# Expert rows packed without gaps: 16 gathers a pass in place of 23, tiles that start at a register's column, and a list of destinations fetched through memory

## The chip, the cores and the metric

The kernel runs on one core of one Trainium2 chip. The metric is the device time in microseconds of one execution. The kernel before takes 743.76 us (median of 3 runs, 742.2 to 744.45).

## The reference

Two sequences (batches) of 1024 rows of 128 numbers pass through six blocks, each with a layer norm in front and a residual after it: experts (344 wide, gated), RWKV time mixing, the same experts again, a second set of experts (512 wide, with biases), retention, and the second set again. Only the expert blocks are touched by the change:

```python
logits = xt @ Ws + bs
topk_w, topk_idx = jax.lax.top_k(logits, K)          # E = 8 experts, K = 2 of them for each row
topk_w = jax.nn.softmax(topk_w, axis=-1)
combine = jnp.sum(jax.nn.one_hot(topk_idx, E) * topk_w[..., None], axis=1)
g = jnp.einsum('td,edf->tef', xt, Wg)
u = jnp.einsum('td,edf->tef', xt, Wu)
y = jnp.einsum('tef,efd->ted', jax.nn.silu(g) * u, Wd)
out = jnp.einsum('ted,te->td', y, combine)
```

The kernel computes only the two chosen experts of each row: 2 x 1024 pairs of row and expert in each batch.

## The kernel before

Four expert blocks (f = 0, 2, 3, 5) times two batches (b) make eight **passes**, numbered 0 to 7: (0,0), (0,1), (2,0), (2,1), (3,0), (3,1), (5,0), (5,1). Passes 0 to 3 are of the gated kind (k = 0), 4 to 7 of the other (k = 1). A pass sorts the 2048 pairs by expert and cuts them into **tiles** of 128 places with one expert each. Each expert begins a new tile, so that a pass needs up to 16 + 7 = 23 tiles (`TILES`), some of whose places are empty.

- **Routing** (`route`, mostly VectorE): logits, the two best experts, a running count, a slot for each pair. A one-hot product on TensorE (step `inv`) turns "pair to slot" into "slot to row". VectorE makes three lists of it: `te` (the expert of each tile), `take_from` (the row for each place) and `send_to` (where each result goes in DRAM; empty places go to spare rows there).
- **Gathering**: GpSimd issues one indirect DMA for each tile (`rows_in`, L1089), DRAM `rows_in` to SBUF `xs`. TensorE transposes the rows in groups (`transpose_in`, L562) of 1, 2, 4, 4, 4, 4, 4 tiles, and ScalarE copies each group from PSUM to `xT_kept` (`copy_x`, L872).
- **A tile**: ScalarE copies the tile's weights (`copy_w`, L865), TensorE multiplies up (`project_up`, L590), ScalarE applies silu, and in passes 0 to 3 VectorE multiplies gate and value into `hT` (`product`, L1304). TensorE multiplies down (`project_down`, L602), and two tiles at a time are copied from one PSUM bank to `ys` (`copy_y`: by ScalarE in passes 0 to 3, L899; by VectorE in passes 4 to 7, L1315). `hT`, the gate and the up banks are double, the down bank `ybank` is single.
- **Sending**: one indirect DMA a tile by GpSimd (`rows_out`, L1103) to DRAM `rows_out`. `ys` holds eight tiles. When a pass is all sent, SyncE reads the results back in eight DMAs (`rows_back`, L449), and VectorE adds them to x with the weights `cw` (`add`, L1390).

The batches leapfrog: while the tiles of one batch run, the other's adds, norm, mixing and routing run beside them. Each engine has one fixed order, written out as a string in `TURNS`: each letter is a program of the engine (`a` is always the tiles, but on SyncE and GpSimd), and `a3` means three steps of it. Nothing overtakes anything on an engine: a step whose semaphore is late holds up all that stands behind it. On TensorE, `load_owner` reads the expert of tile j + 2 from `te` into a register at the head of tile j; ScalarE reads it right before it copies the weights:

```python
load_owner(PASSES[p][1], j)
e = act.snap(owners[j % len(owners)], min_val=0, max_val=E - 1)
nc.scalar.activation(w_up[:, n % 2, 0:UP[k]], w_of(k, e, 0, UP[k]), ACT.Copy).then_inc(w_copied, 1)
```

Of the kernel before, what the change touches and what calls it, by code (L numbers as in the profile page):

```python
# [38 lines left out]
assert OPENS[NG] == TILES  # L39
# [47 lines left out]
    "act":  # L87
# [4 lines left out]
    "pool":  # L92
# [4 lines left out]
    "dve":  # L97
# [47 lines left out]
def build_block(nc, x_in, w0_in, w1_in, cols_in, sq_in, gn_in, const_in, bconst_in, bias_in, rope_in, decay_in, out):  # L145
    ctx = ExitStack()
    with ctx:
# [9 lines left out]

        x = sb("x", [P, NB * NT, P])
# [16 lines left out]
        xnT = sb("xnT", [P, NB, 1 + S])  # L175
        zT = sb("zT", [P, NB, S])
# [12 lines left out]
        gap = sb("gap", [P, 2, NT])  # L189
        tiles_i = sb("tiles_i", [P, E], I32)  # L190
        tiles = sb("tiles", [P, 3, E])
# [6 lines left out]
        of_tile = sb("of_tile", [P, K * NT, NSB], F16)  # L198
        from_row = sb("from_row", [P, K * NT, NSB], F16)
        unused = hot = sb("unused", [P, NSB])  # L200
        row_i = sb("row_i", [P, NSB], I32)
        take_from = sb("take_from", [P, NB, NSB], I32)
        send_to = sb("send_to", [P, NB, NSB], I32)
        count = sb("count", [P, P + K * NT + NSB])
# [170 lines left out]
        def group_after(p, j):  # L375

            q, t = place(p, j)
            if t != max(0, filled(q % NG) - 2) or q % NG == NG - 1 and p in DRAINED:
                return None
# [1363 lines left out]
```

## Time and profile before

| | |
|---|---|
| the profiled execution | 741.35 us, its span 739.4 us, mean granted TensorE clock 0.925 |
| runs | 742.2, 743.76, 744.45 us |
| TensorE (PE) busy | 607.4 us, 82% of the span |
| ScalarE (ACT), GpSimd (POOL), VectorE (DVE) busy | 424.0, 406.3 and 402.1 us |
| moved by DMA | 51.50 MB, mean 70 GB/s |

Times in the trace count from the start of the span. "idle before <-releaser" on a row is the time in which the engine had nothing to do before it, and what ended that time. `SPq` is SyncE, which only issues DMAs. In the timeline, the second number of an issue is how long the issuing engine was taken, not how long the data were under way; the latter stands in the list of DMA issues.

### The profile page before, as it was taken

The page shows a single profiled execution, that of the slowest core. Times are in us where ns is not written, and L with a number is a line of the kernel's source. Part 1 is how long each engine was busy: PE and PEld are TensorE (multiplying, and loading weights), DVE is VectorE, ACT ScalarE, POOL GpSimd, SP SyncE. Part 2 cuts the span into 40 slices and gives each one's busy share as a digit, 9 for nine tenths or more (in the row PEclk, how much of TensorE's full clock was granted, in tenths as well). Part 3 has the DMA queues.
Part 4 walks back from the last instruction along what each step waited for, and adds up shares of the span by engine and source line. Part 5 has one row for each costly group of instructions (what it writes and reads, how often), then busy time and mean ns, then how long its engine had stood idle before and what let it go on. Part 6 is the DMA issues. An engine that isn't in the chain of part 4 may idle for free.

```text
span 739.4 us, 14790 instructions
## 1 busy us (share of the span) xinstructions
PE 607.4 (82%) x4780; PEld 517.1 (70%) x4780; DVE 402.1 (54%) x1253; ACT 424.0 (57%) x1014; POOL 406.3 (55%) x436
## 2 busy tenths in 40 slices
PE   2489959869496997998998889997439999888891
PEld 1489959569366987997988776665336667678891
DVE  5663236856769771672445334586672576660302
ACT  2156637776269754765867676452227454646870
POOL 2167767633657537766776776322038534326773
PEclk9999989969698999999999999999559999998996
DMA  8842231101310213321421311000311001102423
GB/s 342 319 138 54 53 108 47 33 16 51 96 40 23 45 47 89 97 56 44 112 80 43 111 48 34 8 9 16 89 15 43 26 9 30 51 15 51 137 51 111
DMA packets 42617, 51.50 MB, mean 70 GB/s; under 512 B 7848, under 2 KB 33832, under 8 KB 42416
## 3 DMA queue, kind: packets, MB, share of 16 engines
q0 software_dynamic: 11776, 24.14, 12.5%
q1 hardware_dynamic: 30768, 26.41, 10.9%
q8 instruction: 43, 0.70, 0.4%
q14 instruction: 30, 0.25, 0.1%
HBM read 33.22 MB, written 17.30 MB: 68 GB/s over the span
## 4 chain that ended last, share of the span: by engine, by line
PE 52%; POOL 15%; DVE 10%; issue 9%; ACT 7%; DMA 6%; ACTq 0%; SPq 0%; POOLq 0%; DVEq 0%
PE bank L590 19%; PE bank L602 11%; POOL xs L1089 9%; POOL rows_out L1103 7%; PE bank L692 5%; DMA xs<-rows_in,take_from 3%; PE bank L714 2%; PE bank L562 2%; PE bank L670 2%; PE bank L527 2%; DVE in_tile L1266 2%; DMA rows_out<-ys,send_to 1%; PE bank L516 1%; ACT xn L822 1%; ACT L822 1%
## 5 line engine op out<-in xcount | busy, mean ns | idle before, releaser
L590 PE MATMUL bank<-xT_kept,w_up 128*128 128x128 f32 x1840 | 257.5, 290 | 25.5 <-ACT gate L880 8.6
L1103 POOL DMA_INDIRECT rows_out<-ys,send_to x184 | 182.4, 991 | 151.4 <-DVE ys L1315 58.1
L590 PEld LDWEIGHTS bank<-xT_kept,w_up 128*128 128x128 f32 x1840 | 234.1, 202 | 40.1 <-issue 29.7
L1089 POOL DMA_INDIRECT xs<-rows_in,take_from x184 | 180.9, 983 | 126.3 <-issue 49.3
L602 PE MATMUL bank<-w,hT 128*128 x1288 | 182.6, 283 | 14.9 <-DVE ys L1315 8.6
L602 PEld LDWEIGHTS bank<-w,hT 128*128 128x128 f32 x1288 | 164.5, 197 | 24.1 <-issue 23.8
L865 ACT ACTIVATE w_up<-w 128x728 f32 (+1 forms) x184 | 133.0, 725 | 28.1 <-DVE cw L1290 7.6
L887 ACT ACTIVATE hT<-bank,tile_bias 128x128 f32<-128x128 f32 x368 | 104.9, 370 | 45.2 <-PE bank L590 43.4
L1304 DVE TENSOR_TENSOR hT<-gate,bank 128x384 f32<-128x384 f32 x92 | 50.4, 550 | 86.2 <-ACT gate L880 53.2
L872 ACT ACTIVATE xT_kept<-bank 128x512 f32<-128x512 f32 (+2 forms) x56 | 29.2, 522 | 78.9 <-PE bank L562 78.8
L1315 DVE COPY ys<-bank 128x256 f32<-128x256 f32 (+1 forms) x48 | 19.7, 411 | 97.8 <-PE bank L605 81.8
L1539 DVE TENSOR_TENSOR kept<-bank,decay 128x512 f32<-128x512 f32 x64 | 41.4, 685 | 38.1 <-PE bank L692 38.1
L880 ACT ACTIVATE gate<-bank 128x384 f32<-128x384 f32 x92 | 44.4, 483 | 17.1 <-PE bank L590 15.1
L562 PE MATMUL bank<-const,xs 128*128 128x128 f32 x184 | 33.9, 297 | 21.8 <-DMA xs<-rows_in,take_from 21.5
L1390 DVE SCALAR_TENSOR_TENSOR x<-yg,cw,x 128x128 f32<-128x128 f32 x128 | 37.4, 340 | 25.5 <-DMA yg<-rows_out 25.4
L506 PE MATMUL bank<-const,xn 128*128 128x128 f32 x96 | 22.2, 339 | 22.1 <-DVE xn L1191 21.3
L562 PEld LDWEIGHTS bank<-const,xs 128*128 128x128 f32 x184 | 23.1, 152 | 24.3 <-issue 16.2
L692 PE MATMUL bank<-kept 32*128 32x512 f32 x128 | 37.0, 640 | 0.0
L899 ACT ACTIVATE ys<-bank 128x256 f32<-128x256 f32 (+1 forms) x48 | 17.9, 373 | 31.2 <-PE bank L602 30.8
L506 PEld LDWEIGHTS bank<-const,xn 128*128 128x128 f32 x96 | 14.5, 166 | 27.5 <-issue 20.5
L822 ACT ACTIVATE kept<-bank 128x128 f32<-128x128 f32 (+1 forms) x36 | 12.0, 332 | 33.2 <-PE bank L681 21.9
L1167 DVE BATCH_NORM_STATS2 stats<-x 128x6 f32<-128x128 f32 x96 | 26.1, 277 | 8.4 <-DMA colv<-in_vectors 6.3
(160 smaller groups left out, 708.1 us busy)
## 6 DMA issues: line engine op xcount, KB each, us to landing
yg<-rows_out SPq DMA_DIRECT2D x64, 128.0 KB, 2.9
w<-in_w SPq DMA_DIRECT2D x8, 536.0 KB, 10.4
rows_in<-xn SPq DMA_DIRECT2D x16, 256.0 KB, 2.4
w<-in_w SPq DMA_DIRECT2D x8, 512.0 KB, 8.7
xs<-rows_in,take_from POOLq DMA_INDIRECT x184, 3.0
rows_out<-ys,send_to POOLq DMA_INDIRECT x184
x<-in_x SPq DMA_DIRECT2D x2, 512.0 KB, 5.6
decay<-in_decay SPq DMA_DIRECT2D x1, 1024.0 KB, 13.2
```

What stands on the lines that cost most here:

```text
L562: last = nc.tensor.transpose(xT[:, t * P:(t + 1) * P], xs[:, q % 2, t, :], ident)
L590: last = mm(to, w_up[:, n % 2, start_col:start_col + P], rows_in, start=True, stop=True)
L602: last = mm(y, hT[0:n_f, n % 2, c * P:(c + 1) * P], w_of(k, e, WD[k] + c * P, P, n_f), start=(c == 0), stop=(k == 0 and c == CH[k] - 1))
L692: mm(to[:], r_kT[quad, c % 2, :], r_qm[quad, c % 2, :, :].rearrange("p a b -> p (a b)"), start=True, stop=True).then_inc(RE_PE.sem, 1)
L865: nc.scalar.activation(w_up[:, n % 2, 0:UP[k]], w_of(k, e, 0, UP[k]), ACT.Copy).then_inc(w_copied, 1)
L880: nc.scalar.activation(gate[:, n % 2, :], bank[0][:, 0:CH[0] * P], ACT.Silu).then_inc(gate_ready, 1)
L887: last = nc.scalar.activation(hT[:, n % 2, c * P:(c + 1) * P], bank[up_bank(p, j)][:, c * P:(c + 1) * P], ACT.Silu, bias=own)
L1089: pool.indirect_dma_start(xs[:, q % 2, t, :], None, xn_dram[b], own).then_inc(ld_xs[q % 2][t], 16)
L1103: pool.indirect_dma_start(y_dram[b], own, ys[:, m % 4 // 2, m % 2 * 2 + j % 2, :], None)\
L1304: V.tensor_tensor(hT[:, n % 2, 0:CH[0] * P], gate[:, n % 2, :], bank[up_bank(p, j, 1)][:, 0:CH[0] * P], ALU.mult)\
L1390: V.scalar_tensor_tensor(row, yg[:, s, t, :], cw[:, b, s, t:t + 1], row, ALU.mult, ALU.add)\
L1539: step(V.tensor_tensor(r_A[:, c % 2, q * HALF:(q + 1) * HALF], score[q % 2][:], decay[:, q * HALF:(q + 1) * HALF], ALU.mult))
```

## The change

1. **No gaps.** Slots are counted without rounding each expert up, so the 2048 pairs of a pass fill exactly 16 blocks of 128 rows (`ROWS`): 16 gathers a pass, and groups of 1, 3, 4, 4, 4. `xT_kept` goes. ScalarE copies each transposed group into `turned`, 2048 columns and 128 zeros behind them for each batch, in the place of `xnT` and `zT`.
2. **Tiles stay at 23**, but overlap blocks: the tile's 128 columns begin where a new list `off` says. TensorE reads `off` into a register beside `te`, and `project_up` takes `turned[:, b, register : register + 128]`. A pass's tiles wait for `off`, made some steps after `te`.
3. **Destinations.** `send_to` can no longer be read off `inv` in tile order. VectorE writes the rows of the 16 blocks out as numbers (`row_f`), TensorE transposes them (a fourth routing step, `turn`), VectorE copies the result (`row_t`), SyncE writes it to DRAM (`place_dram`), waits, and then for each of the 23 tiles reads `off` into a register and issues a DMA of 128 numbers of 4 bytes, one for each partition, into `places[:, b, j]`. VectorE waits for all 23 and makes `send_to` of them with two operations.
4. **Routing on VectorE** loses three small operations ahead of the slots and gets some fifteen behind them. `gap`, `hot` and `unused` are double by batch.
5. **The orders** of all five engines are written anew.

```diff
-GROUPS = [1, 2] + [GRP] * ((TILES - 3) // GRP)
+ROWS = K * S // P
+GROUPS = [1, 3] + [GRP] * ((ROWS - 4) // GRP)
...
     "sp":
-        "a3 c3 a2 b9 a2 b8 a2 b8 a2 b8 a2 b16 a4 b8 d5 b8 d4",
+        "a3 d3 a2 b5 c9 a2 c8 b2 a2 b2 c8 a2 b2 c8 a2 b2 c16 a2 b2 a2 b2 c8 e5 c8 e4",
...
+            def places_by_tile():
+                for p, (f, b) in enumerate(PASSES):
+                    steps = RT_DVE[b]
+                    yield
...
+                    sp.wait_ge(steps.sem, steps.done(SUB[f], "row_t"))
+                    sp.dma_start(place_dram[b][1:1 + K * S].rearrange("(t p) -> t p", p=P), row_t[0:ROWS, b, :]).then_inc(places_out[b], 16)
+                    yield
...
+                    sp.wait_ge(places_out[b], 16 * (SUB[f] + 1))
+                    for j in range(TILES):
+                        own = offs[j % len(offs)]
+                        sp.reg_load(own, off[0:1, b * NSB + j:b * NSB + j + 1])
+                        first = sp.snap(own, min_val=1, max_val=1 + K * S)
+                        sp.dma_start(places[:, b, j:j + 1], place_dram[b][bass.ds(first, P)].unsqueeze(1)).then_inc(places_back[b], 16)
...
             def load_owner(b, j):
                 pe.reg_load(owners[j % len(owners)], te[0:1, b * NSB + j:b * NSB + j + 1])
+                pe.reg_load(offs[j % len(offs)], off[0:1, b * NSB + j:b * NSB + j + 1])
...
-                if t == 0:
-                    pe.wait_ge(xT_copied, q + 1)
+                if j in OPENS[0:NG]:
+                    pe.wait_ge(xT_copied, p * NG + OPENS.index(j) + 1)
                 pe.wait_ge(w_copied, n + 1)
-                rows_in = xT_kept[:, q % 2, t * P:(t + 1) * P]
+                first = pe.snap(offs[j % len(offs)], min_val=1, max_val=1 + K * S)
+                rows_in = turned[:, PASSES[p][1], bass.ds(first, P)]
...
-                    for j in range(TILES):
+                    for j in range(ROWS):
                         yield
                         q, t = place(p, j)
...
-                step(V.scalar_tensor_tensor(send_to[:, b, :], row_i[:], 0.0, unused[:], ALU.add, ALU.add))
+                step(V.scalar_tensor_tensor(unused[:, b, :], full[:, b, :], 0.0, count[:, P + K * NT:], ALU.is_equal, ALU.mult))
+                yield
+
+                dve.wait_ge(places_back[b], 16 * TILES * (v + 1))
+                after(R, v, "unused")
+                step(V.tensor_tensor(full[:, b, :], full[:, b, :], places[:, b, :], ALU.mult))
+                after(R, v, "kept")
+                step(V.tensor_tensor(send_to[:, b, :], full[:, b, :], unused[:, b, :], ALU.add))
                 yield
```

The orders of VectorE, spelled out from the new string around the two steps that matter (`row_t` is the copy that lets SyncE write the list; `SEND` is the wait for all 23 DMAs with its two operations; P3.1 is the product of tile 1 of pass 3, Y4.10 the copy of the eleventh pair of pass 4, A a step of adding, N the norm):

| pass | what stands between `row_t` and `SEND` | what follows `SEND` |
|---|---|---|
| 0 | set-up, first steps of the next routing, P0.0, P0.1 | next routing, P0.2 |
| 1 | P0.10, set-up, P0.11, P0.12 | P0.13 |
| 2 | ten adds, P2.0, P2.1, a norm, P2.2 | P2.3, RWKV of batch 1 |
| 3 | P2.22, P3.0 | P3.1 |
| 4 | P3.21, P3.22 | residual, A of pass 3 (four steps), Y4.0 |
| 5 | Y4.9 | Y4.10 |
| 6 | two adds, a norm | residual, first rotation of retention of batch 1 |
| 7 | Y6.10, Y6.11 | residual, Y7.0 |

`row_t` itself follows the routing closely (passes 0, 2, 6, 7: right behind `take_from` and `off`; pass 3: behind P2.20 and P2.21; pass 5: behind Y4.8; pass 1: behind P0.8 and P0.9; pass 4: behind P3.19 and P3.20). In GpSimd's new order the sends of a pass begin behind 12 to 16 of its gathers, as they began behind 11 to 15 before.

## Rows read from the trace of the kernel before

**Rows 1.** The page: chain that ended last, and costliest groups (busy us, mean ns)
```profile
PE bank L590 19%; PE bank L602 11%; POOL xs L1089 9%; POOL rows_out L1103 7%; PE bank L692 5%; DMA xs<-rows_in,take_from 3%; PE bank L714 2%; PE bank L562 2%; PE bank L670 2%; PE bank L527 2%; DVE in_tile L1266 2%; DMA rows_out<-ys,send_to 1%; PE bank L516 1%; ACT xn L822 1%; ACT L822 1%
...
L1103 POOL DMA_INDIRECT rows_out<-ys,send_to x184 | 182.4, 991 | 151.4 <-DVE ys L1315 58.1
...
L1089 POOL DMA_INDIRECT xs<-rows_in,take_from x184 | 180.9, 983 | 126.3 <-issue 49.3
...
L562 PE MATMUL bank<-const,xs 128*128 128x128 f32 x184 | 33.9, 297 | 21.8 <-DMA xs<-rows_in,take_from 21.5
```

**Rows 2.** Timeline of POOL, the last send of pass 0
```profile
98.73 0.97 POOL L1103 DMA_INDIRECT rows_out<-ys,send_to  x1 [0.30 <-issue]
```

**Rows 3.** Busy time by stretch: PE, PEld, DVE, ACT, POOL, clock, DMA share, GB/s
```profile
100.00:110.00 10.00, 4.96 (x22) 4.12 (x23) 4.72 (x19) 1.79 (x3) 6.83 (x7) 0.66 0.57 158
```

**Rows 4.** Timeline of SP: start, us for all of them, count
```profile
28.48 0.44 SPq L462 DMA_DIRECT2D decay<-in_decay  x1
...
101.12 3.95 SPq L449 DMA_DIRECT2D yg<-rows_out  x8
...
353.62 4.58 SPq L449 DMA_DIRECT2D yg<-rows_out  x8
```

**Rows 5.** DMA issues: KB each, median us from issue to landing
```profile
rows_in<-xn SPq DMA_DIRECT2D x16, 256.0 KB, 2.4
...
decay<-in_decay SPq DMA_DIRECT2D x1, 1024.0 KB, 13.2
```

**Rows 6.** Timeline of DVE, then ACT: the list te, and the copy that reads it
```profile
543.61 0.17 DVE L1276 TENSOR_SCALAR te<-owner 128x24 int32<-128x24 f32 x1
...
544.23 0.63 ACT L865 ACTIVATE w_up<-w 128x512 f32 x1 [7.50 <-DVE te L1276]
```

**Rows 7.** Timeline of DVE at the start of pass 0
```profile
31.61 0.18 DVE L1283 TENSOR_SCALAR take_from<-row_i 128x24 int32<-128x24 int32 x1
...
45.30 0.55 DVE L1304 TENSOR_TENSOR hT<-gate,bank 128x384 f32<-128x384 f32 x1 [0.91 <-PE bank L590]
...
49.65 0.55 DVE L1304 TENSOR_TENSOR hT<-gate,bank 128x384 f32<-128x384 f32 x1
```

**Rows 8.** Timeline of DVE in pass 0, the first and last of six products
```profile
62.20 0.55 DVE L1304 TENSOR_TENSOR hT<-gate,bank 128x384 f32<-128x384 f32 x1 [1.31 <-PE bank L590]
...
73.00 0.55 DVE L1304 TENSOR_TENSOR hT<-gate,bank 128x384 f32<-128x384 f32 x1 [1.69 <-ACT gate L880]
```

**Rows 9.** Timeline of DVE at the starts of passes 2 and 3
```profile
191.23 0.18 DVE L1283 TENSOR_SCALAR take_from<-row_i 128x24 int32<-128x24 int32 x1
...
209.21 0.55 DVE L1304 TENSOR_TENSOR hT<-gate,bank 128x384 f32<-128x384 f32 x1 [2.42 <-ACT gate L880]
...
275.25 0.18 DVE L1283 TENSOR_SCALAR take_from<-row_i 128x24 int32<-128x24 int32 x1
...
286.76 0.56 DVE L1304 TENSOR_TENSOR hT<-gate,bank 128x384 f32<-128x384 f32 x1 [3.60 <-PE bank L590]
```

**Rows 10.** Timeline of DVE around the starts of passes 4 and 5
```profile
337.93 0.56 DVE L1304 TENSOR_TENSOR hT<-gate,bank 128x384 f32<-128x384 f32 x1 [0.26 <-ACT gate L880]
...
354.14 0.42 DVE L1315 COPY ys<-bank 128x256 f32<-128x256 f32 x1 [11.63 <-PE bank L605]
...
398.17 0.18 DVE L1283 TENSOR_SCALAR take_from<-row_i 128x24 int32<-128x24 int32 x1
...
405.65 0.42 DVE L1315 COPY ys<-bank 128x256 f32<-128x256 f32 x1 [3.43 <-PE bank L605]
```

**Rows 11.** Timeline of DVE around the starts of passes 6 and 7
```profile
545.99 0.18 DVE L1283 TENSOR_SCALAR take_from<-row_i 128x24 int32<-128x24 int32 x1
...
557.10 0.76 DVE L1530 TENSOR_TENSOR kept<-bank,rope 128x256 f32<-128x256 f32 x2 [4.96 <-PE bank L670]
...
663.42 0.18 DVE L1283 TENSOR_SCALAR take_from<-row_i 128x24 int32<-128x24 int32 x1
...
679.29 0.42 DVE L1315 COPY ys<-bank 128x256 f32<-128x256 f32 x1 [4.80 <-PE bank L605]
```

More of the change, by code:

```diff
@@ L156, in build_block @@
         y_dram = [nc.dram_tensor(f"rows_out{b}", [K * S + NSB * P, P], F32).ap() for b in range(NB)]
+        place_dram = [nc.dram_tensor(f"places{b}", [1 + K * S + P], I32).ap() for b in range(NB)]
         x = sb("x", [P, NB * NT, P])
@@ L197, in build_block @@
         in_tile = sb("in_tile", [P, K * NT, P], F16)
[L198 to L202, printed above, removed]
+        of_tile = sb("of_tile", [P, K * NT, ROWS], F16)
+        from_row = sb("from_row", [P, K * NT, ROWS], F16)
+        unused = hot = sb("unused", [P, NB, NSB])
+        full = sb("full", [P, NB, NSB])
+        none_of = sb("none_of", [P, E + 1])
+        reach = sb("reach", [P, NSB, E])
+        row_i = sb("row_i", [P, ROWS], I32)
+        row_f = sb("row_f", [P, ROWS])
+        row_t = sb("row_t", [P, NB, P], I32)
+        places = sb("places", [P, NB, NSB], I32)
+        take_from = sb("take_from", [P, NB, ROWS], I32)
         send_to = sb("send_to", [P, NB, NSB], I32)
@@ L307, in build_block @@
                         ["lg", "top0", "eq0", "nth0", "pick0", "rest", "top1", "eq1", "nth1", "pick1", "sel", "carry",
-                         "gap", "tile127", "tiles_i", "tiles", "end", "start", "slot", "mine", "pos", "slot_i", "tile", "in", "eq", "rows", "in0", "in1",
-                         "ended", "owner", "te", "unused", "row_i", "take", "send", "w0", "w1"]) for b in range(NB)]
+                         "gap", "end", "start", "slot", "mine", "pos", "slot_i", "tile", "in", "eq", "rows", "in0", "in1",
+                         "tile127", "tiles_i", "tiles", "last", "ended", "owner", "te", "row_i", "take", "row_f",
+                         "none", "pad", "ahead", "padded", "less", "at", "off", "row_t", "more", "sum", "reach", "full", "unused", "kept", "send",
+                         "w0", "w1"]) for b in range(NB)]
         RES = [Steps(sem(f"res{b}"), [f"res{i}" for i in range(NH)]) for b in range(NB)]
@@ L375, in group_after @@
         def group_after(p, j):
-            q, t = place(p, j)
-            if t != max(0, filled(q % NG) - 2) or q % NG == NG - 1 and p in DRAINED:
-                return None
-            return q + 1
-        def last_tile(q):
-            return q // NG * TILES + OPENS[q % NG + 1] - 1
+            if j == TILES - 2 and p not in DRAINED:
+                return (p + 1) * NG
+            for g in range(1, NG):
+                if j == max(OPENS[g] - 2, OPENS[g - 1]):
+                    return p * NG + g
+            return None
         def up_made(n, part=0):
@@ L484, in _ @@
             owners = [pe.alloc_register(f"owner{i}") for i in range(6)]
+            offs = [pe.alloc_register(f"off{i}") for i in range(4)]
             ident = const[:, K_ID:K_ID + P]
@@ L519, in route @@
                 own = 6 if (f, b) == (5, 0) else 7
-                to = take(own, RT_DVE[b], v, "send")
+                to = take(own, RT_DVE[b], v, "more")
                 for t in range(NT):
@@ L855, in route @@
                 after(RT_DVE[b], v, "gap")
[L856 removed]
+                run(gap[:, b, 1, :], gap[:, b, 0, :], ACT.Tanh, RT_ACT[b], scale=0.5)
             def copy_w(p, j):
@@ new lines, in route @@
+                yield
+                step(V.tensor_tensor(none_of[:, 0:E], start_of, end_of, ALU.subtract))
+                after(R, v, "none")
+                step(V.scalar_tensor_tensor(pad_of, tiles_of, float(P), none_of[:, 0:E], ALU.mult, ALU.add))
+                after(R, v, "pad")
+                step(V.tensor_tensor(more_of, pad_of, none_of[:, 1:E + 1], ALU.subtract))
+                step(V.tensor_tensor(reach[:, :, :], ended[:, :, :], pad_of.unsqueeze(1).to_broadcast([P, NSB, E]), ALU.mult))
@@ new lines, in route @@
+                after(R, v, "padded")
+                after(R, v, "te")
+                step(V.tensor_reduce(owner[:], reach[:, :, :], AX.X, ALU.add))
+                after(R, v, "less")
+                step(V.scalar_tensor_tensor(owner[:], const[:, K_J:K_J + NSB], float(P), owner[:], ALU.mult, ALU.subtract))
+                after(R, v, "at")
+                step(V.tensor_scalar(off[:, b * NSB:(b + 1) * NSB], owner[:], float(K * S), 1.0, ALU.min, ALU.add))
+                yield
+                after(RT_PE[b], v, "turn")
@@ L1284, in route @@
+                step(V.tensor_copy(row_t[0:ROWS, b, :], own[0:ROWS, 320:320 + P]))
                 if k == 1:
                     V.tensor_copy(tile_bias[:, b, :, :], heads(own[:, 192:192 + CH[1] * NSB], CH[1], NSB)).then_inc(TB_DVE[b].sem, 1)
-                step(V.scalar_tensor_tensor(send_to[:, b, :], row_i[:], 0.0, unused[:], ALU.add, ALU.add))
+                step(V.tensor_tensor(reach[:, :, :], ended[:, :, :], more_of.unsqueeze(1).to_broadcast([P, NSB, E]), ALU.mult))
+                after(R, v, "more")
@@ new lines, in route @@
+                step(V.tensor_reduce(owner[:], reach[:, :, :], AX.X, ALU.add))
+                after(R, v, "sum")
+                step(V.scalar_tensor_tensor(owner[:], const[:, K_J:K_J + NSB], -float(P), owner[:], ALU.mult, ALU.add))
+                after(R, v, "reach")
+                step(V.tensor_scalar(full[:, b, :], owner[:], none_of[:, 0:1], count[:, P:P + 1], ALU.subtract, ALU.is_ge))
+                after(R, v, "full")
+                step(V.scalar_tensor_tensor(unused[:, b, :], full[:, b, :], 0.0, count[:, P + K * NT:], ALU.is_equal, ALU.mult))
@@ L1289, in route @@
                 for s, sign in enumerate((0.25, -0.25)):
-                    step(V.tensor_scalar(cw[:, b, s, :], gap[:, 1, :], sign, 0.25, ALU.mult, ALU.add))
+                    step(V.tensor_scalar(cw[:, b, s, :], gap[:, b, 1, :], sign, 0.25, ALU.mult, ALU.add))
                 if k == 1:
```

101 lines of the change are left out of this document (61 added, 40 removed), and 39 rows, old and new, of the table TURNS.

## Prediction

> **What bounds the kernel now.** I read the page first. TensorE is busy for 82% of the span and no other engine for more than 57%, but the chain that ended last gives the tiles' matmuls only 30% and GpSimd's two indirect DMAs 16% [rows 1]. A gather or a send costs GpSimd 0.98 or 0.99 us [rows 1] and 0.30 us before the next, 1.27 us in a row [rows 2]; a pass has 46 of them, 58 us, against some 50 us of tile work on TensorE (23 tiles at 2.16 us: the six products between 62.20 and 73.00 lie five tiles apart [rows 8]). So GpSimd falls behind in a pass without other work, and the next pass's gathers come late: between 100 and 110 us TensorE works 4.96 of 10 us and its granted clock is 0.66 in place of 1 [rows 3]. The reader is to see two things: GpSimd's backlog is real but hurts only at the ends of passes, and the tiles run on a pace of about 2 us, set by TensorE with ScalarE and VectorE in the loop. Whatever stops VectorE for longer than one tile stops the tiles (its product fills `hT`, or its copy frees the single `ybank`).
>
> **What the change takes away.** 56 of 184 gathers: 56 x 1.27 = 71 us of GpSimd. Of this only what lies on the chain counts. Gathers have 9% of the chain, 66 us, and 56/184 of that is 20; transposes have 2%, 15 us, and 56/184 of that is 4.5 [rows 1]. Together **24 us gained**. The bounds: the gap at 100 to 110 us alone, 5 us [rows 3], and all 71 us. I take 24, since TensorE is close to full outside such gaps. The copies to `turned` are fewer than those to `xT_kept`, but ScalarE waits beside TensorE. The lost operations ahead of the slots (three of some 0.2 us, as `te` with its gap [rows 6]) are given back by the four of `te` that moved behind `in1`; `off` comes some 1.7 us behind `take_from`, while the first tile waits for a gather, a transpose and a copy anyway: nothing, and 1.7 us a pass if that cover were gone.
>
> **What it adds: the way of the destinations.** From `row_t` to `SEND` this stands in a row, and nothing of it overlaps:
> - the write to DRAM, from issue to landing: 2.4 us, as the stores of `rows_in` [rows 5];
> - 23 times a register load and a DMA issue on SyncE. Eight issues take 3.95 us [rows 4], 0.49 us each. These have static addresses. The load: `te` ends at 543.78 and ScalarE, which waits for it, reads it into a register and starts its copy at 544.23 [rows 6], 0.45 us with the semaphore and the start, so about 0.4. The load and the issue that needs it are in order on one queue, so I take 0.9 us an entry: 0.4 + 22 x 0.9 = 20.2 us to the last issue. The bounds: 0.49 (the load hidden behind the issue), and 1.25 (a slower load, and arithmetic of a dynamic address, which no row shows);
> - the last one's landing: 2.4 us by the same row.
>
> The sum is **25 us from `row_t` to `SEND`**, 16 by the lower bound, 33 by the upper. The rows show a register load of about 0.4 us on ScalarE [rows 6]. The Trainium skill, "DMA: Bandwidth & Descriptors", section "Latency and other measured facts", puts a tensor_load at a floor of about 600 ns; with that an entry would be 1.09 us, the way 29 us, and the total below some 30 us higher.
>
> What is queued behind it: VectorE's wait for all 23 DMAs stands in its one order, a few steps behind `row_t`. Behind it stand the products and copies of the running pass, for which TensorE waits within one or two tiles, and GpSimd's sends. How much each pass loses is the time at which its next step can run, less the time at which it ran before:
> - **Pass 0**: `take_from` is done at 31.8 [rows 7], `row_t` about 33.5. The list is on SyncE's queue behind the weights of the other experts and `decay`, issued at 28.48 and landed 13.2 us later, 41.7 [rows 4, 5]. The write lands behind them, about 42; 42 + 20.2 + 2.4 = 64.6, P0.2 at some 65.5 in place of 49.65 [rows 7]: 16 us.
> - **Pass 1**: three products, 6.5 us by [rows 8], lie between `row_t` and `SEND`; P0.13 would be due 2.2 us later: 25 - 8.7 = 16 us.
> - **Pass 2**: `take_from` + 2 + 25 = 27 us; P2.3 came at 209.21, 18 us behind 191.23 [rows 9]: 9 us.
> - **Pass 3**: + 2.5 + 25 = 27.5; P3.1 came 11.5 us behind `take_from` [rows 9]: 16 us.
> - **Pass 4**: `row_t` behind P3.20 (337.93 [rows 10]), so `SEND` at 363.5. SyncE reads pass 3 back only behind its list, at 361 in place of 353.62 [rows 4], and Y4.0 stands behind four of those adds: 367 in place of 354.14 [rows 10]: 13 us. TensorE idled for a part of those 12 us before as well.
> - **Pass 5**: + 3 + 25 = 28; Y4.10 came 7.5 us behind `take_from` [rows 10]: 20.5 us. Pass 4's last sends, its reading back and so retention of batch 0 come as much later.
> - **Pass 6**: + 2 + 25, and 1.5 for the residual = 28.5; the first rotation of retention came 11.1 us behind `take_from` [rows 11]: 17.5 us.
> - **Pass 7**: 28.5 as well; Y7.0 came 15.9 us behind [rows 11]: 12.5 us.
>
> The sum is 16 + 16 + 9 + 16 + 13 + 20.5 + 17.5 + 12.5 = **120.5 us lost**. They add, since each stops tiles or the chain of the next routing, and all eight lie one behind the other in time. Parts that I cost at nothing: the second register load a tile on TensorE (0.4 us x 184 = 74 us if its queue runs dry, and the tile pace of rows 8, which has one such load, leaves no gap), the tile's start at an odd column, and 2,944 packets of 4 bytes a pass, 184 for each of 16 DMA engines in 20 us. VectorE's some fifteen small operations at 0.2 us are 3 us a pass, mostly beside waits. GpSimd's sends start up to 10 us later than its order has them, but its 39 DMAs (50 us) fit into a pass that is now longer.
>
> **Sum**: 120.5 - 24 = 96.5 us on the profiled execution's 741.35: 838 us. The median of the runs shown is 2.4 us above that execution: **840 us**. A change of 0.3% (2.2 us) is about what a measurement of this kernel can tell from none.
>
> **The rivals.**
> - *The load hides behind the issue* (25%). SyncE's sequencer goes on while an issue is being worked off, an entry costs 0.49, and `SEND` comes 16 us behind `row_t`. Each of the eight losses is 9 us less: 7, 7, 0, 7, 4, 11.5, 8.5, 3.5 = 48.5; less 24 is +25: **768 us**. For it: the issues of 0.49 us show no work of their own in the trace beyond the 0.43 of the issue. Against: the next issue can't form its address before its register is there.
> - *More than forecast* (10%). The entry is 1.25 us or TensorE's second load shows: 7.7 us more in eight places, 62 us: **900 us**.
> - *Faster: the list is short* (12%). The one mechanism that decides the sign is SyncE's time per entry. The new order of VectorE puts `SEND` only 4 to 6 us behind `row_t` (three products in pass 1), which fits a list whose issues cost next to nothing. If small transfers can be handed over at 0.06 us each, `SEND` waits hardly anywhere, and the 24 us remain: **719 us**. It decides below 0.37 us an entry: 96.5/8 = 12 us less of the 25. Against it stands that every issue of SyncE takes 0.44 to 0.57 us whatever its size [rows 4]. By the Trainium skill, same page, section "Anatomy of one DMA", a sequencer hands a DMA over in some 50 ns; that is said of GpSimd's way, and on SyncE this trace has 0.49 us.
> - *The gain is larger* (with the 25% above it would reach no change, 5%): if not 24 but some 50 of GpSimd's 71 us come back, and an entry is 0.49 us, it ends near **743 us**.
>
> **How the numbers follow.** The forecast's own case, an entry of 0.75 to 1.1 us, has 48% and runs from 815 to 880. The range takes in the hidden load and goes up to the upper bound of an entry: 762 to 900, which leaves out the fast list, most of the larger gain, and what lies above 900. Faster: 12% and half of the last, 14%. Same: 3%. Slower: 83%.
>
> **What would show it.** In the new trace's timeline of SP, 23 issues of `places` a pass: their distance is the entry (0.9 us; 0.5 for the first rival; 0.1 for the fast list). VectorE should stand idle before the operation that makes `full` out of `places`, released by the DMA `places`, eight times and some 100 us in all; 16 to 19 us in passes 0 and 1. TensorE should stand in the same stretches at the lower clock. GpSimd should show 128 gathers, idle before the first send of a pass, and no more gap at the start of pass 1 by late gathers. The prediction is wrong if VectorE finds the list there, or if tiles go on while it waits (then the losses don't add), and its size is wrong if entries are not 0.9 us.

## The result and the profile after

The changed kernel takes **847.71 us** (median of 4 runs, 845.68 to 850.25) beside 742.98 us (4 runs, 742.2 to 744.45) for the kernel before on the same chip: ratio **1.141**, 95% interval 1.137 to 1.145. It is slower by 105 us. The forecast was 840 us, its range 762 to 900.

The page of the changed kernel (busy time, clock, the chain that ended last, costliest groups):

```profile
span 845.6 us, 15852 instructions
...
PE 630.9 (75%) x4732; PEld 532.9 (63%) x4732; DVE 422.3 (50%) x1375; ACT 417.7 (49%) x998; POOL 352.3 (42%) x381
...
PE 50%; SPq 17%; DVE 10%; issue 8%; ACT 7%; DMA 6%; ACTq 0%; POOL 0%; POOLq 0%; DVEq 0%
PE bank L634 19%; PE bank L646 13%; SPq L470 8%; SPq L468 6%; PE bank L736 4%; DMA places<-row_t 2%; PE bank L758 2%; ACT hT L932 2%; PE bank L714 2%; DMA places<-places 2%; PE bank L565 1%; DVE in_tile L1310 1%; ACT xn L866 1%; PE bank L60
...
L1149 POOL DMA_INDIRECT rows_out<-ys,send_to x184 | 185.6, 1009 | 289.4 <-DVE ys L1401 116.4
...
L1135 POOL DMA_INDIRECT xs<-rows_in,take_from x128 | 123.6, 966 | 106.5 <-DVE none_of L1339 57.4
...
L1370 DVE TENSOR_TENSOR full<-full,places 128x24 f32<-128x24 f32 x8 | 1.5, 183 | 125.8 <-DMA places<-places 125.8
...
L605 PE MATMUL bank<-const,xs 128*128 128x128 f32 x128 | 24.7, 308 | 6.2 <-DMA xs<-rows_in,take_from 4.8
```

Three things are to be seen beside [rows 1]. GpSimd has left the chain (gathers and sends had 16%, now POOL has 0%), and the transposes wait for gathers for 4.8 us in place of 21.5: what the change was to relieve is relieved. (The list stretches this kernel and so gives GpSimd time as well; the run with one entry a pass, below, shows the same without it, 1% and 4.4 us.) SyncE, which had no share of the chain, has 17%: L468 is the register load of a list entry, L470 its DMA. And one operation of 0.18 us, L1370, which stands behind VectorE's wait for the list, has 125.8 us of idle time ahead of it.

The timeline of SP shows the eight lists (start, us for all 23, count):

```profile
44.36 18.74 SPq L470 DMA_DIRECT2D places<-places  x23
...
85.88 19.06 SPq L470 DMA_DIRECT2D places<-places  x23
...
226.21 18.79 SPq L470 DMA_DIRECT2D places<-places  x23
...
323.02 18.08 SPq L470 DMA_DIRECT2D places<-places  x23
...
395.40 19.54 SPq L470 DMA_DIRECT2D places<-places  x23
...
466.85 18.64 SPq L470 DMA_DIRECT2D places<-places  x23
...
629.56 19.32 SPq L470 DMA_DIRECT2D places<-places  x23
...
764.39 18.60 SPq L470 DMA_DIRECT2D places<-places  x23
```

They sum to 150.8 us, 18.85 a list. From the first issue's start to the last one's end are 22 distances and one issue of 0.33 us: (18.85 - 0.33) / 22 = 0.84 us an entry on average, and 0.81 in the shortest list, the fourth (18.08 us). The chain through pass 1's list shows what an entry is made of (start, us, what):

```profile
84.06 1.37 DMA places<-row_t
85.88 0.34 SPq L470
...
91.28 0.33 SPq L470
91.66 0.32 SPq L468
92.13 0.33 SPq L470
...
104.61 1.97 DMA places<-places
107.16 0.47 DVE hT L1390
```

A load takes 0.27 to 0.32 us and an issue 0.33. From an issue's end to the next load are 0.04 us, from a load's end to its issue 0.16, in which the trace has L469, the `snap` of the register, for 0.04 and a first piece of L470 for 0.03. The next load begins only when the issue has ended. From the write at 84.06 to the last landing at 106.58 are 22.5 us. TensorE in the midst of such a wait (stretch; PE, PEld, DVE, ACT, POOL busy; clock, DMA share, GB/s):

```profile
100.00:110.00 10.00, 2.23 (x10) 2.23 (x11) 1.44 (x6) 0.51 (x2) 0.00 (x0) 0.50 0.05 1
```

TensorE works 2.23 of 10 us, at a granted clock of 0.50, the lower of its two levels (1.2 GHz), and GpSimd does nothing. In pass 0 the order of VectorE behind the list reads:

```profile
64.75 0.18 DVE L1370 TENSOR_TENSOR full<-full,places 128x24 f32<-128x24 f32 x1 [17.67 <-DMA places<-places]
64.97 0.18 DVE L1372 TENSOR_TENSOR send_to<-full,unused 128x24 int32<-128x24 f32 x1
...
66.51 0.55 DVE L1390 TENSOR_TENSOR hT<-gate,bank 128x384 f32<-128x384 f32 x1
```

The forecast had `SEND` (L1370 and L1372) at 64.6 and P0.2 (L1390) at 65.5. That it fits so well is in part luck: the first issue came at 44.36, 2 us later than forecast (42.4), and the list and its landing were 1.8 us shorter. `row_t` was ready at 33.1, but SyncE wrote it only at 37.61, since an issue ahead of it (L458, the zeros behind the list in DRAM, which the forecast left out) held SyncE for 3.67 us.

### The profile page after: what moved, and what is told of

Its sections match the earlier page's. It is cut to its first block, busy times and chain, and to the rows that moved or that the text cites. A ratio compares the mean times of both kernels' runs of the same rounds, so it can differ in the third digit from the quotient of the medians.

```text
span 845.6 us, 15852 instructions
## 1 busy us (share of the span) xinstructions
PE 630.9 (75%) x4732; PEld 532.9 (63%) x4732; DVE 422.3 (50%) x1375; ACT 417.7 (49%) x998; POOL 352.3 (42%) x381
## 4 chain that ended last, share of the span: by engine, by line
PE 50%; SPq 17%; DVE 10%; issue 8%; ACT 7%; DMA 6%; ACTq 0%; POOL 0%; POOLq 0%; DVEq 0%
PE bank L634 19%; PE bank L646 13%; SPq L470 8%; SPq L468 6%; PE bank L736 4%; DMA places<-row_t 2%; PE bank L758 2%; ACT hT L932 2%; PE bank L714 2%; DMA places<-places 2%; PE bank L565 1%; DVE in_tile L1310 1%; ACT xn L866 1%; PE bank L605 1%; PE bank L554 1%
## 5 line engine op out<-in xcount | busy, mean ns | idle before, releaser
L1149 POOL DMA_INDIRECT rows_out<-ys,send_to x184 | 185.6, 1009 | 289.4 <-DVE ys L1401 116.4
L634 PE MATMUL bank<-turned,w_up 128*128 x1840 | 269.8, 298 | 34.9 <-ACT gate L925 11.4
L634 PEld LDWEIGHTS bank<-turned,w_up 128*128 128x128 f32 x1840 | 242.7, 208 | 56.9 <-issue 55.1
L646 PE MATMUL bank<-w,hT 128*128 x1288 | 193.2, 294 | 76.6 <-DVE ys L1401 37.9
L646 PEld LDWEIGHTS bank<-w,hT 128*128 128x128 f32 x1288 | 175.3, 208 | 84.8 <-issue 84.1
L1135 POOL DMA_INDIRECT xs<-rows_in,take_from x128 | 123.6, 966 | 106.5 <-DVE none_of L1339 57.4
L1390 DVE TENSOR_TENSOR hT<-gate,bank 128x384 f32<-128x384 f32 x92 | 50.2, 551 | 71.0 <-PE bank L634 41.8
L1370 DVE TENSOR_TENSOR full<-full,places 128x24 f32<-128x24 f32 x8 | 1.5, 183 | 125.8 <-DMA places<-places 125.8
L917 ACT ACTIVATE turned<-bank 128x512 f32<-128x512 f32 (+2 forms) x40 | 20.6, 514 | 75.0 <-PE bank L605 69.4
L1176 POOL TENSOR_TENSOR kept<-kept 128x256 f32<-128x256 f32 x16 | 11.6, 726 | 58.2 <-DVE kept L1619 58.1
L605 PE MATMUL bank<-const,xs 128*128 128x128 f32 x128 | 24.7, 308 | 6.2 <-DMA xs<-rows_in,take_from 4.8
```

Source lines behind the costliest of these rows:

```text
L634: last = mm(to, w_up[:, n % 2, start_col:start_col + P], rows_in, start=True, stop=True)
L646: last = mm(y, hT[0:n_f, n % 2, c * P:(c + 1) * P], w_of(k, e, WD[k] + c * P, P, n_f), start=(c == 0), stop=(k == 0 and c == CH[k] - 1))
L1135: pool.indirect_dma_start(xs[:, q % 2, t, :], None, xn_dram[b], own).then_inc(ld_xs[q % 2][t], 16)
L1149: pool.indirect_dma_start(y_dram[b], own, ys[:, m % 4 // 2, m % 2 * 2 + j % 2, :], None)\
L1390: V.tensor_tensor(hT[:, n % 2, 0:CH[0] * P], gate[:, n % 2, :], bank[up_bank(p, j, 1)][:, 0:CH[0] * P], ALU.mult)\
```

## The experiments

Twelve runs were made, in three groups, each group with the kernel before on the same chip. The first group's chip gave 741.61 us for the kernel before (median of 13), beside 742.98 in the first measurement. The other two groups fell on two other chips, on which the kernel before takes 881.44 us (median of 7) and 882.92 us (median of 11). Times are therefore compared within a group only, with one exception: the changed kernel did not run in the first group, and its 847.71 us are taken from the first measurement, where the kernel before differs by 0.2%. "The first chip" below means both.

The kernels with fixed addresses, with one entry a pass and with fixed columns leave out the destinations: `send_to` is a fixed count in them, so that results go to consecutive rows of DRAM and not to their own. With fixed columns the tiles hold other rows too. The others compute all.

### First group: what the list costs

**Fixed addresses.** The list's DMAs stay, the load of the register goes, and with it the address made of it:

```diff
-                        own = offs[j % len(offs)]
-                        sp.reg_load(own, off[0:1, b * NSB + j:b * NSB + j + 1])
-                        first = sp.snap(own, min_val=1, max_val=1 + K * S)
-                        sp.dma_start(places[:, b, j:j + 1], place_dram[b][bass.ds(first, P)].unsqueeze(1))...
+                        first = 1 + j % ROWS * P
+                        sp.dma_start(places[:, b, j:j + 1], place_dram[b][first:first + P].unsqueeze(1))...
...
-                step(V.tensor_tensor(send_to[:, b, :], full[:, b, :], unused[:, b, :], ALU.add))
+                step(V.tensor_scalar(send_to[:, b, 0:TILES], count[:, P:P + TILES], -1.0, None, ALU.add))
```

> The 23 DMAs of the list have fixed addresses, with no register load in front of them; VectorE still waits for all 23. The destinations are then not the tiles' own: the sends go to fixed rows, so the output is scrambled. Theory (an entry of the list, now 0.82 us, is a register load and an issue one behind the other, and every microsecond of it is paid in each of eight passes): the entry falls to the 0.49 us of the other issues, each wait is 7.2 us shorter, the time falls by some 57 us to about 790 us. Rival (the handing over of small DMAs is slow by itself): entries stay at 0.8 us and the time at 848 us.

Measured: 789.17 us, ratio 1.065 (1.056 to 1.074), 58.5 us below the changed kernel. VectorE's wait, from the view of waits (us in total, times, longest):

```profile
DVE full L1368 <- DMA places<-places: 68.6, 8, 11.8
```

Its eight lists sum to 93.1 us, 57.7 fewer than the 150.8 (an issue every 0.51 us: 11.63 less 0.43, over 22), and the kernel is 58.5 us faster: what a list gains the kernel gains, one for one, and the fixed destinations, which this run has as well, are left with at most 1 us. The register load does not hide behind the issue.

**One entry a pass.** `range(TILES)` becomes `range(1)`, VectorE waits for that one, and the destinations are fixed as in the run before:

```diff
-                    for j in range(TILES):
+                    for j in range(1):
...
-                dve.wait_ge(places_back[b], 16 * TILES * (v + 1))
+                dve.wait_ge(places_back[b], 16 * (v + 1))
```

> The list is one DMA a pass in place of 23; destinations fixed as in the first run, so the output is scrambled. All else of the change stays: packed gathers, the transposes, the write to memory and its landing, VectorE's added operations. Theory: of the 125.8 us that VectorE waits, each wait loses up to 18 us, so nearly all; what remains is the gain by 56 fewer gathers, about 24 us: some 720 to 725 us, faster than the kernel before. Rival (a part of the loss is the added operations or the second register load of TensorE): it ends above 743 us.

Measured: 740.37 us (10 runs), ratio 0.999 (0.995 to 1.003). VectorE's wait for the list is 3.0 us in all. Without the rest of the list the whole change makes no difference that can be measured. The other 22 entries of the eight lists cost 847.7 - 740.4 = 107.3 us, and the gain of the packing, forecast at 24 us, is missing: the 720 to 725 us expected here did not come.

**The list twice.** 46 entries a pass, the second half into a second buffer, and VectorE waits for all:

```diff
-                    for j in range(TILES):
+                    for i, j in enumerate([*range(TILES), *range(TILES)]):
...
-                        sp.dma_start(places[:, b, j:j + 1], ...
+                        sp.dma_start((places, places2)[i >= TILES][:, b, j:j + 1], ...
...
-                dve.wait_ge(places_back[b], 16 * TILES * (v + 1))
+                dve.wait_ge(places_back[b], 16 * 2 * TILES * (v + 1))
```

> The list is fetched twice (46 DMAs, the second 23 into a tile that nobody reads), and VectorE waits for all 46. Theory: 23 x 0.82 = 18.7 us more in each of eight passes, all of it added: 150 us more, about 998 us. Rival (passes overlap or other waits absorb a part): clearly under 120 us more.

Measured: 998.22 us, ratio 1.347, 150.5 us above the changed kernel. Its eight lists sum to 301.3 us, 150.5 more than the changed kernel's: the same number. The view of waits:

```profile
DVE full L1371 <- DMA places<-places: 275.7, 8, 38.1
```

149.9 us more than the 125.8. Nothing absorbs even a part of the second half. Of the first half a little is absorbed: from one entry to 23 the lists grow by 147.8 us and the kernel by 107.3, so that some 5 us a list cost nothing, and every entry beyond is on the path.

**The wait on GpSimd.** VectorE no longer waits. GpSimd waits for the list just ahead of the first send of a pass, and makes `send_to` itself with four small operations, in place of VectorE's:

```diff
-                dve.wait_ge(places_back[b], 16 * TILES * (v + 1))
-                after(R, v, "unused")
-                step(V.tensor_tensor(full[:, b, :], full[:, b, :], places[:, b, :], ALU.mult))
...
+                            pool.wait_ge(places_back[b], 16 * TILES * (SUB[f] + 1))
+                            nc.gpsimd.tensor_copy(place_f[:, b, :], places[:, b, :])...
+                            nc.gpsimd.tensor_tensor(full[:, b, :], full[:, b, :], place_f[:, b, :], ALU.mult)...
+                            nc.gpsimd.tensor_tensor(full[:, b, :], full[:, b, :], unused[:, b, :], ALU.add)...
+                            nc.gpsimd.tensor_copy(send_to[:, b, :], full[:, b, :])...
```

> The wait for the list and the making of send_to move from VectorE to GpSimd, right in front of a pass's first send; the list is as slow as before, and every order stays. Theory (what costs is that VectorE's products and copies stand behind the wait): tiles run on while the list is fetched, eight of them find room; GpSimd's gathers and retention steps behind its first send still come late, some 5 to 10 us in passes 0, 5 and 6: 750 to 775 us. Rival (the late destinations hold up the sends and so the pass, whoever waits): 830 us or more.

Measured: 778.47 us, ratio 1.052 (1.044 to 1.060). The lists are as long as before:

```profile
44.38 18.96 SPq L472 DMA_DIRECT2D places<-places  x23
```

So 69 of the 107 us are owed to who waits for the list: VectorE's wait stops products and copies that have nothing to do with destinations. 38 us stay, and GpSimd waits 42.3 us for the list. The time lies 3.5 us above the upper end of the expected 750 to 775.

### Second group: finer waits, and TensorE's second load

**The list in three parts** (8, 8 and 7 entries), each with its own semaphore, and GpSimd waits for a part at the first send that uses it:

```diff
-                        ....then_inc(places_back[b], 16)
+                        ....then_inc(places_part[b][j // 8], 16)
...
+                        if j % 8 == 0:
+                            pool.wait_ge(places_part[b][c], 16 * (min(j + 8, TILES) - j) * (SUB[f] + 1))
```

> As the wait on GpSimd, which measured 778.5 us and let GpSimd wait 42 us for lists, but the list is taken in three parts of 8, 8 and 7 entries: GpSimd waits for the first eight before the first send, 2.4 + 8 x 0.82 + 2.4 = 11 us behind row_t in place of 24. Theory: the wait of GpSimd all but vanishes and the time comes to that of the one-entry list and some small operations: 742 to 752 us. Rival (SyncE's queue being full is the cost: reading back stands behind the list): it stays at 765 us or more.

Measured: 851.40 us beside 881.44, ratio 0.966 (0.961 to 0.971). GpSimd's wait for the list is down to 6.8 us, once, and SyncE has 4% of the chain. The wait all but vanished, as the theory had it; the expected times were those of the first chip and can't be set beside this one. The time does not come to that of one entry a pass, which is 822 to 826 us on this chip with fixed columns.

**A fixed column, without and with the second load** (both have one entry a pass). TensorE reads its tiles from fixed columns. The first drops the load of `off` (the line taken out below), the second keeps it and doesn't use it:

```diff
-                pe.reg_load(offs[j % len(offs)], off[0:1, b * NSB + j:b * NSB + j + 1])
...
-                first = pe.snap(offs[j % len(offs)], min_val=1, max_val=1 + K * S)
-                rows_in = turned[:, PASSES[p][1], bass.ds(first, P)]
+                first = 1 + j % ROWS * P
+                rows_in = turned[:, PASSES[p][1], first:first + P]
```

> The one-entry list (740.4 us), and TensorE's tiles start at fixed columns, with no second register load a tile; the output is scrambled. The one-entry run gained 2 us in place of the 24 expected of the packed gathers; its trace shows 82 short stops of TensorE's weight loads ahead of the up products, 55 us in all, where the kernel before had 42 and 30 us. Theory A (the second register load costs TensorE 0.1 to 0.2 us a tile): 715 to 725 us. Theory B (what ate the gain is VectorE's fifteen added operations in the routing, and the order): 738 to 741 us.

> As the run before, but TensorE still loads the second register for each tile and does not use it. Theory A (the load costs, not the column that starts at an odd place): 740 us. Rival (reading from a register's column costs): as fast as the run without load.

Measured: 822.18 us without the load, ratio 0.933 (0.928 to 0.939), and 826.02 us with it, 0.936 (0.931 to 0.941). The intervals overlap: the 3.8 us between the two are within the noise, and the 184 loads don't cost 74.

**Four loads ahead of four issues** on SyncE, in the otherwise unchanged new kernel:

```diff
+                        for j in some:
+                            sp.reg_load(offs[j % len(offs)], off[0:1, b * NSB + j:b * NSB + j + 1])
+                        for j in some:
+                            first = sp.snap(offs[j % len(offs)], min_val=1, max_val=1 + K * S)
+                            sp.dma_start(places[:, b, j:j + 1], ...
```

> The changed kernel whole, with one edit: SyncE loads four registers in a row and then issues their four DMAs, in place of load, issue, load, issue. Theory (loads run one into the next, and four cost little more than one, 0.33 us): an entry falls from 0.82 to some 0.57 us, 23 entries by 5.6 us, the time by 8 x 5.6 = 45 us to about 803 us. Rival (each load takes its 0.33 us wherever it stands): 848 us.

Measured: 919.50 us, ratio 1.043 (1.037 to 1.049). The trace shows why the expected 45 us didn't come: where nothing disturbs SyncE, four loads start at 103.77, 104.07, 104.36 and 104.66 us, 0.30 apart, their four issues at 105.10, 105.62, 106.14 and 106.65, 0.52 apart, and the next load at 107.02. Four entries take 3.25 us, the same 0.81 us each. The changed kernel itself had not run on a chip of this speed, so it did in the next group.

### Third group: the open sizes on one chip

> The changed kernel itself, beside the others of this call, so that all are compared on one chip. Theory (the list costs 0.815 us an entry on the path): 1.141 times the kernel before, as in the first measurement (848 us beside 743). Where the chip is one on which the kernel before takes about 881 us, the run with four loads ahead of four issues had 1.043; the changed kernel should stand at 1.04 to 1.06 there.

> The changed kernel with one list entry a pass and fixed destinations for the scatters (the rows land in other places than the reference's). Theory (packing the tiles is worth about 2 us and the list all the rest): 0.997 to 1.003 times the kernel before, 740 us where that takes 742. Rival (packing is worth more and the first run of it missed it): 0.97 to 0.98.

> As the run before, and TensorE reads each tile from a fixed column, with no second register load (so the tiles hold other rows too). Theory (the register's column costs TensorE little, as the 4 us between the two runs with and without the load say): 0.5% below the run before, 736 us. Rival (a start in an odd or register-given column slows each transpose, and this took the 24 us that the packing was forecast to give): 3% below, about 718 us. The run tells the two apart, since it differs from the one before in nothing else.

> The whole change computed in full, with the list in three parts (8, 8 and 7 entries) that GpSimd waits for just ahead of the scatters that use them, and SyncE's register loads four ahead of four issues. Theory (VectorE's wait is gone, and what stays is SyncE's and GpSimd's own path): the run with the wait on GpSimd for all 23 had 778 us; by thirds the first scatter waits for 8 entries and not 23, 12 us less in each of 7 passes at most, of which GpSimd shows 42 us of wait in all: 742 to 760 us, 1.00 to 1.025 times the kernel before. With the loads by four an entry costs no less if the 0.815 us are 0.49 of issue and 0.33 of load one after the other (22 x 0.815 = 18 us a list); rival: the loads overlap, and a list takes 22 x 0.5 = 11 us, which would put the time near 740.

The edits are those above; the last one joins the three parts and the loads by four.

| kernel | us | ratio to the kernel before (882.92) | 95% |
|---|---|---|---|
| changed | 920.76 | 1.041 | 1.035 to 1.046 |
| one entry a pass | 826.49 | 0.938 | 0.934 to 0.942 |
| the same, fixed columns, no second load | 827.62 | 0.936 | 0.931 to 0.940 |
| three parts on GpSimd, loads by four | 853.15 | 0.966 | 0.961 to 0.971 |

What follows:
- Loads by four are worth nothing that can be measured: 1.043 beside 1.041, and 0.966 with them beside 0.966 without, each pair on two chips of the same speed. Load and issue add up in either order.
- The register's column and the second load cost TensorE nothing in time (826.49 and 827.62). They do leave a trace: the short stops "issue" ahead of the weight loads of the up products are 87.9 us with the column from a register and 66.3 with a fixed one. On the first chip they are 29.7 us in the kernel before and 55.2 with one entry a pass; there no run had fixed columns, so that a cost of the register's column is not excluded where the 24 us are missing.
- The list costs 920.76 - 826.49 = 94 us here, much as the 107 us on the first chip. Moved to GpSimd in parts it costs 853.15 - 826.49 = 27. Of these GpSimd waits 7.0 us for the list, and its own small operations keep it busy for 24 us more (378.3 beside 353.9); what the rest is was not separated. The run came out below its expected ratio of 1.00 to 1.025, which took the first chip's times for its base.
- The forecast of 0.997 to 1.003 for one entry a pass failed, and so did its rival's 0.97 to 0.98. The same kernel that equals the kernel before on the first chip is 6% faster than it here.

The last point is about the chips. One entry a pass, on the first chip and on this one, from the two pages and views of waits. First chip:

```profile
span 738.6 us, 15148 instructions
...
L634 PE MATMUL bank<-turned,w_up 128*128 x1840 | 264.7, 294 | 34.7 <-ACT gate L925 11.8
L1135 POOL DMA_INDIRECT xs<-rows_in,take_from x128 | 124.4, 972 | 95.2 <-DVE none_of L1339 56.0
```

This chip:

```profile
span 822.6 us, 15148 instructions
...
PE 59%; DVE 11%; ACT 10%; issue 8%; another core or an unknown queue 7%; DMA 3%; POOL 1%; ACTq 1%; SPq 0%; DVEq 0%; POOLq 0%
...
L634 PE MATMUL bank<-turned,w_up 128*128 x1840 | 277.0, 303 | 65.1 <-issue 23.7
...
L1135 POOL DMA_INDIRECT xs<-rows_in,take_from x128 | 124.5, 972 | 114.8 <-DVE none_of L1339 59.4
...
PEld bank L634 <- issue: 87.9, 90, 6.0
...
DVE hT L1390 <- remote: 35.3, 7, 6.7
ACT hT L932 <- remote: 33.7, 8, 7.7
DVE ys L1401 <- remote: 31.5, 6, 8.7
```

A gather takes 972 ns on both and VectorE's product 552, but TensorE's work is longer, an up product 303 ns beside 294, at a mean clock of 0.90 beside 0.92: in all it is busy for 640.1 us in place of 611.8, 28 of the 84 us by which the span is longer. The rest is waits to which the trace gives no plain releaser: "remote", 149 us on all engines together and absent on the first chip, and "issue", 87.9 us in place of 55.2 ahead of L634's weight loads. SyncE shows such stops too; in pass 1 of the changed kernel on this chip the chain has 0.26 to 0.28 us for most loads, but in one burst

```profile
93.15 0.52 issue
93.71 0.68 SPq L468
94.42 0.72 SPq L470
```

so its eight lists sum to 184.2 us in place of 150.8. What holds the engines up there, and why the kernel before loses 140 us to it and one entry a pass only 86, is open: no trace of the kernel before was taken on such a chip.

## Why the prediction was right, and where it was not

**The list is on the path, 25 us from `row_t` to `SEND`: right, a little too high.** Measured in pass 1: 1.4 for the write, 0.4 to the first issue, 18.7 of issues, 2.0 for the landing, 22.5 in all. The entry was 0.84 us on average, not 0.9: with a fixed address it is 0.51, and load and register address add 0.33. The forecast load was 0.4; the trace shows 0.27, then 0.16 us with the register up to the issue, and an issue with an address from a register is recorded at 0.33 us where one with a fixed address has 0.43. The Trainium skill's floor of about 600 ns for a tensor_load ("DMA: Bandwidth & Descriptors", section "Latency and other measured facts") would have made the entry 1.09 us, by the prediction's estimate; SyncE's load here is 0.27 us, so the measurement decides against it. The 50 ns that the Trainium skill gives for handing a DMA over (same page, "Anatomy of one DMA") is said of GpSimd's way; SyncE has 0.33 to 0.43 us.

**"They add, since each stops tiles or the chain of the next routing": right.** 120.5 us were forecast, 107.3 measured. The entry's error, 22 x 0.06 x 8 = 11 us, is most of the difference in the sum; the passes by themselves missed in both directions. Where the time went follows from when SyncE begins to read each pass back, one entry a pass against the full list (timeline of SP; both on the first chip):

| stretch that ends with pass | lists in it | one entry, us | changed, us | more | forecast |
|---|---|---|---|---|---|
| 0 | 0, 1 | 100.1 | 135.0 | 34.9 | 32 |
| 1 | none | 83.3 | 83.5 | 0.2 | 0 |
| 2 | 2, 3 | 108.2 | 122.8 | 14.6 | 25 |
| 3 | 4 | 57.8 | 73.9 | 16.1 | 13 |
| 4 | 5 | 63.1 | 78.3 | 15.2 | 20.5 |
| 5 to 7 | 6, 7 | 316.1 | 341.8 | 25.7 | 30 |

They sum to 106.7 us. The largest miss is at passes 2 and 3, 10 us less than forecast; passes 0 and 1 and pass 4 lose 3 us more each, pass 5 and passes 6 and 7 some 5 less each. The shorter entry accounts for 1.3 us a list; what remains of the misses nearly cancels, and that it does is luck.

**24 us gained by packing: the term that was mis-sized.** On the first chip some 1 us came out of it (740.4 beside 741.6), and by the interval of the ratio (0.995 to 1.003) at most 3.4. The engines' shares of the chain, before and with one entry a pass, show what took the place of the gathers:

```profile
PE 52%; POOL 15%; DVE 10%; issue 9%; ACT 7%; DMA 6%; ACTq 0%; SPq 0%; POOLq 0%; DVEq 0%
...
PE 68%; DVE 12%; ACT 9%; issue 6%; DMA 3%; POOL 1%; SPq 1%; ACTq 0%; DVEq 0%; POOLq 0%
```

GpSimd's 15% went to 1%, and the kernel is as long as before: TensorE has 68% of the chain in place of 52. It is busy for 611.8 us in place of 607.4, and VectorE, with the added steps of routing, for 422.7 in place of 402.1. Stretch by stretch (ends of passes as above; columns as in [rows 3]) the kernel before has

```profile
101.12:189.66 88.54, 71.89 (x486) 62.87 (x486) 60.32 (x163) 55.58 (x88) 47.33 (x45) 0.87 0.18 50
189.66:290.78 101.12, 82.42 (x575) 72.19 (x576) 68.05 (x186) 64.68 (x103) 59.99 (x58) 0.89 0.20 51
290.78:353.62 62.84, 59.78 (x501) 56.98 (x500) 32.36 (x110) 41.47 (x84) 44.65 (x46) 0.97 0.29 75
...
415.28:687.08 271.80, 231.81 (x1895) 172.18 (x1893) 154.32 (x465) 139.03 (x433) 123.04 (x146) 0.91 0.13 37
687.08:729.55 42.47, 33.71 (x295) 32.45 (x293) 8.39 (x26) 27.98 (x84) 31.44 (x32) 0.97 0.32 90
```

and one entry a pass has

```profile
100.08:183.38 83.30, 69.52 (x482) 59.65 (x480) 61.78 (x165) 54.25 (x85) 38.77 (x35) 0.91 0.15 45
183.38:291.57 108.19, 88.25 (x580) 77.58 (x581) 71.10 (x214) 65.27 (x103) 54.77 (x53) 0.86 0.16 45
291.57:349.36 57.79, 53.49 (x443) 50.07 (x442) 34.63 (x124) 35.24 (x67) 33.49 (x34) 0.97 0.23 68
...
412.43:690.91 278.48, 238.28 (x1921) 178.06 (x1919) 160.18 (x497) 141.19 (x440) 112.89 (x136) 0.90 0.12 33
690.91:728.53 37.62, 32.56 (x277) 30.27 (x275) 8.06 (x25) 26.04 (x80) 22.23 (x23) 1.00 0.27 85
```

The stretches that end with passes 1, 3 and 7 are 5.2, 5.1 and 4.9 us shorter, with pass 0's 1.0 some 16 us, and the gap of [rows 3] is gone (TensorE works 9.26 of the 10 us from 100 to 110, at a clock of 1.00). Passes 2, 4, and 5 with 6 are 7.1, 1.4 and 6.7 us longer and give it back. In the two of these shown the granted clock is lower as well (0.86 beside 0.89, 0.90 beside 0.91), TensorE is busy for 6 us more in each, and VectorE for 3 and 6 us more. But the stretches don't hold the same work: that of pass 3 has 443 matmuls in place of 501, and only seven of these are transposes that the packing saves, while that of passes 5 and 6 has 26 more. So a part of the 16 us, and of what is given back, is work that moved across the end of a pass, and how much the closed gaps are worth by themselves is not shown.

The forecast took what vanishes from the chain as gained, and counted the edits that can lengthen it (the new orders, the added routing steps, the column from a register) at nothing. That step failed: 24 us were forecast and some 1 was measured. Which of the edits takes the place of the gathers is open. No run had the old orders with the packed rows, and fixed columns ran only on the slower chips.

**Costed at nothing, and rightly:** the 4-byte packets (the last list entry of pass 1 lands 1.97 us behind its issue, and the list's time is load and issue). Rightly as far as the slower chips show: the second register load on TensorE (3.8 us between two runs on one chip, within the noise) and the odd and register-given column (nothing that can be measured, on the other).

**The rivals:** the hidden load (768) fell with the entry of 0.84 us in the new trace, and with fixed addresses, which took 58.5 us away. The fast list (719) fell with the same 0.84 us against its deciding 0.37, and even with one entry a pass the kernel ends at 740. "More than forecast" (900) wanted an entry of 1.25 us or a second load that shows, and had neither. The larger gain fell on the first chip. On the two others the change without its list gains 6%, which no term of the prediction held.

**Where it nets out by luck.** 840 against 848 looks closer than it is: the loss was 13 us too high, the gain some 22 us too high, and the first hid part of the second.

**A version that beats both, on two chips of three.** Three parts on GpSimd has 0.966 of the kernel before on the two slower chips, with the full computation. On the first chip it was not run; with all 23 entries waited for at once it had 1.052 there. So none was shown that beats the kernel before on every chip. With its loads by four it beats the changed kernel by 7% on one of the slower chips (853.15 beside 920.76).

## What to carry to other kernels

Of a list of small DMAs that one engine hands out, multiply entries by the time of load plus issue (0.84 us here) before anything else: bytes did not matter (with a fixed address an entry of 0.5 KB took SyncE 0.51 us and one of 128 KB 0.49 [rows 4]), and neither did the order of loads and issues. Put the wait for such a list on the engine that uses it, as late as it can stand and in parts: the same lists cost 107 us waited for by VectorE and 38 by GpSimd (on another chip 94, and 27 by GpSimd in parts). And when work is taken off an engine that has a share of the chain, price the orders and steps that come with it by a run without the suspected cost: shares of the chain say what vanishes, not what takes its place.

## What the runs showed of the hardware that was not expected

- SyncE does not overlap a register load (0.27 us) with an issue (0.33 us), nor do four loads in a row help (0.30 us each, then 0.52 an issue).
- An issue with an address from a register is recorded shorter (0.33 us) than one with a fixed address (0.43 us), though 23 of the former with their loads take 18.8 us and 23 of the latter 11.6.
- Chips differ: the kernel before takes 742 us on one and 881 and 883 us on two others, and the change's ratio is 1.141 on the first and 1.041 on one of the others. A ratio from one chip did not carry over.
